# Linear attention and a mixture of experts on one core: the values' product folded into the heads' matrix

## The reference

```
q = xn @ Wq + bq;  k = xn @ Wk + bk;  v = xn @ Wv + bv
q = heads(q @ Wq2 + bq2);  k = heads(k @ Wk2 + bk2);  v = heads(v @ Wv2 + bv2)   # 16 heads of 8
q = elu(q) + 1;  k = elu(k) + 1
S = einsum('bhld,bhle->bhde', k, q)
out = einsum('bhmd,bhde->bhme', v, S)
qks = einsum('bhld,bhld->bhl', q, k) + 1e-6
out = out / qks[..., None]
out = layernorm(xn + out @ Wo + bo) * gamma + beta
# experts: 64 of them, 8 per token, at most 160 tokens each, and a shared one; swiglu with 384 inner units
logits = xn @ wg.T;  w, idx = top_k(softmax(logits), 8);  w /= sum(w)
y = sum over the chosen e of w_e * (x1 * silu(x2)) @ w2_e.T,  [x1, x2] = xn @ w1_e.T
```

## Time and profile before

| | |
|---|---|
| median of 3 runs | 354.65 us (354.23 to 355.87) |
| profiled execution's own time | 355.68 us |
| its span in the trace | 353.8 us |
| busy | PE 328.9 us (93%), DVE 281.6 (80%), ACT 194.8 (55%), POOL 251.5 (71%) |
| chain that ended last | PE 81%, DVE 8%, ACT 3%, issue 3%, DMA 2% |
| granted TensorE clock, mean | 0.992 |
| TensorE waits of L1280 (`up`) | 0.4 us in all, in g = 0, for the copy L609 of ScalarE |

### The profile page before, as it was taken

One profiled execution on the slowest core, in us unless ns is written; L12 is line 12 of the kernel. 1 busy time (PEld: TensorE's weight loads), 2 busy tenths in 40 slices (PEclk: granted clock), 3 DMA queues, 4 the chain that ended last, 5 costly groups with the idle time before them and its releaser, 6 DMA issues.

```text
span 353.8 us, 8965 instructions
## 1 busy us (share of the span) xinstructions
PE 328.9 (93%) x2944; PEld 314.2 (89%) x2944; DVE 281.6 (80%) x1134; ACT 194.8 (55%) x433; POOL 251.5 (71%) x258
## 2 busy tenths in 40 slices
PE   8899766999999999999999999999999999998880
PEld 8889665999999999999999999999999999997870
DVE  3898996887798989888888888898989886652595
ACT  3789622746565665757474746565665757343110
POOL 5687826158878878887888888877878886786200
PEclk9999999999999999999999999999999999999996
DMA  7997552499887778787868777887778787834598
GB/s 211 355 383 244 141 120 76 161 324 264 192 221 179 200 177 223 165 215 192 204 168 210 166 205 188 185 219 182 199 169 230 157 229 172 216 44 36 155 318 252
DMA packets 57054, 70.29 MB, mean 199 GB/s; under 512 B 11952, under 2 KB 44976, under 8 KB 57008
## 3 DMA queue, kind: packets, MB, share of 16 engines
q1 hardware_dynamic: 39536, 55.55, 50.4%
q0 software_dynamic: 15360, 13.12, 24.1%
q10 hardware_dynamic: 2112, 1.05, 1.0%
HBM read 54.26 MB, written 15.43 MB: 197 GB/s over the span
## 4 chain that ended last, share of the span: by engine, by line
PE 81%; DVE 8%; ACT 3%; issue 3%; DMA 2%; POOL 1%; SPq 1%; DVEq 0%; POOLq 0%
PE bank L1280 30%; PE bank L1290 12%; PE bank L1215 9%; PE bank L1224 5%; PE bank L1325 4%; PE bank L1299 4%; PE bank L1365 3%; PE bank L1331 2%; PE bank L1371 2%; PE bank L1346 2%; PE bank L1338 2%; PE bank L1254 1%; PE bank L1306 1%; DVE left L791 1%; PE bank L1239 1%
## 5 line engine op out<-in xcount | busy, mean ns | idle before, releaser
L515 POOL DMA_INDIRECT acc<-ys,idx_g x64 | 102.7, 1605 | 30.5 <-issue 15.4
L1280 PE MATMUL bank<-xe,ew 128*128 128x160 f32 x768 | 116.3, 301 | 0.4 <-ACT xe L609 0.4
L1280 PEld LDWEIGHTS bank<-xe,ew 128*128 128x128 f32 x768 | 107.4, 190 | 1.7 <-ACT xe L609 0.6
L496 POOL DMA_INDIRECT gath<-xng,idx_g x80 | 81.2, 1015 | 30.5 <-issue 27.3
L582 ACT ACTIVATE si<-bank 128x480 f32<-128x480 f32 (+1 forms) x96 | 52.1, 543 | 66.7 <-PE bank L1280 38.0
L1290 PE MATMUL bank<-ew,ac 128*128 128x128 f32 x384 | 53.4, 275 | 0.4 <-issue 0.4
L1290 PEld LDWEIGHTS bank<-ew,ac 128*128 128x128 f32 x384 | 49.5, 192 | 1.6 <-issue 0.8
L1215 PE MATMUL bank<-xT,shw 128*128 128x128 f32 x384 | 48.8, 276 | 0.1
L771 DVE TENSOR_TENSOR ac<-si,bank 128x480 f32<-128x480 f32 x64 | 40.9, 640 | 8.6 <-ACT si L582 5.2
L1215 PEld LDWEIGHTS bank<-xT,shw 128*128 128x128 f32 x384 | 45.6, 192 | 0.5 <-ACT si L582 0.3
L1224 PE MATMUL bank<-shw,acs 128*128 128x128 f32 x192 | 27.7, 280 | 6.8 <-DVE acs L762 4.1
(11 more groups left out here) (165 smaller groups left out, 613.5 us busy)
## 6 DMA issues: line engine op xcount, KB each, us to landing
ew<-in_expert_w SPq DMA_DIRECT2D x64, 384.0 KB, 3.6
ew<-in_expert_w SPq DMA_DIRECT2D x64, 192.0 KB, 2.9
ew<-acc SPq DMA_DIRECT2D x8, 512.0 KB, 7.9
x_sb<-in_x SPq DMA_DIRECT2D x8, 256.0 KB, 6.5
xng<-xn SPq DMA_DIRECT2D x8, 256.0 KB, 4.1
acc<-zeros SPq DMA_DIRECT2D x4, 512.0 KB, 4.3
acc<-betas SPq DMA_DIRECT2D x4, 512.0 KB, 3.0
gath<-xng,idx_g POOLq DMA_INDIRECT x80, 3.8
```

Of the source, the lines that this page charges most:

```text
L496: pool.indirect_dma_start(out=gath[:, p, m, :], out_offset=None, in_=xng, in_offset=bass.IndirectOffsetOnAxis(ap=idx_g[:, g % 4, m:m + 1], ...
L515: pool.indirect_dma_start(out=acc[adds_to[g, m]], out_offset=bass.IndirectOffsetOnAxis(ap=idx, axis=0), in_=src, in_offset=None, compute_o ...
L1280: last = pe.matmul(h_view(n, half_ + 1, CAP)[:, c, :], ew[p][m][:, k * P:(k + 1) * P], xe[:, p, m, :], start=True, stop=True)
```

## The change

The kernel no longer computes v. With C = Wv' S (Wv' the folded weights of v, S the heads' matrix) and c = S^T bvc, the attention output before the scaling, turned, is C^T xn^T + c. `fold_heads` therefore turns the inverses (which are spread to 8 columns for each head beforehand, `rq` of 128x256), multiplies `S_s` by the bias column and by the folded weights, all into `AV` (385 columns), and ScalarE's `heads_copy` takes them to `rC_s` in one copy. `attention_out` is then one product of 256 columns, and VectorE's scale adds c and multiplies by the turned inverses, writing `oT_s` directly. `values`, `out_T` and their two copies are gone. The folded value weights are stored turned. Places in the orders of TensorE, ScalarE and VectorE change with it.

```diff
-            def values_copy(a):
-
-                act.wait_ge(v_full, v_at['values', a] + 1)
-                if a > 0:
-                    act.wait_ge(q_full, q_at['out', a - 1] + 1)
-                act.activation(vT[:, :], AV[:, 0:L], ACT.Identity, bias=bvc[:, 0:1]).then_inc(v_done, 1)
-
-            def out_copy(a):
-
-                act.wait_ge(v_full, v_at['out T', a] + 1)
-                if a > 0:
-                    act.wait_ge(q_full, q_at['project', a - 1] + 1)
-                act.activation(oT_s[:, :], AV[:, 0:L], ACT.Copy).then_inc(v_done, 1)
+            def heads_copy(a):
+
+                act.wait_ge(v_full, v_at['fold', a] + 1)
+                act.activation(rC_s[:, :], AV[:, 0:L + D + 1], ACT.Copy).then_inc(v_done, 1)
...
             cum_copy(NR - 1)
-            values_copy(0)
             load_silu()
             silu(('s', 4))
             silu(('s', 5))
+            heads_copy(0)
+            silu(('s', 6))
             narrow_copy(1)
-            silu(('s', 6))
-            out_copy(0)
             silu(('s', 7))
...
-                if attend:
-                    values_copy(g + 1)
                 y_copy(g, 0)
...
                 silu(('s', EARLY + g))
+                if attend:
+                    heads_copy(g + 1)
                 if g + 2 < NG:
                     narrow_copy(g + 2)
                 silu(('e', g, 3))
-                if attend:
-                    out_copy(g + 1)
...
-                dve.reciprocal(rq[:, :, :], qks[:, :, :]).then_inc(rq_ready, 1)
+                if a > 0:
+                    dve.wait_ge(v_full, v_at['fold', a - 1] + 1)
+                dve.reciprocal(rq[:, :].rearrange("p (n d) -> p n d", d=DH),
+                               qks[:, :, :].rearrange("p j h -> p (j h)").unsqueeze(2).to_broadcast([P, TB * H, DH])).then_inc(rq_ready, 1)
...
                 dve.wait_ge(q_full, q_at['out', a] + 1)
-                dve.wait_ge(rq_ready, a + 1)
-                if a > 0:
-                    dve.wait_ge(v_full, v_at['out T', a - 1] + 1)
-                dve.tensor_tensor(o_s[:, :, :].rearrange("p j (h d) -> p (j h) d", h=H),
-                                  AQ[:, 0:TB * D].rearrange("p (n d) -> p n d", d=DH),
-                                  rq[:, :, :].rearrange("p j h -> p (j h)").unsqueeze(2).to_broadcast([P, TB * H, DH]),
-                                  ALU.mult).then_inc(q_done, 1)
+                dve.wait_ge(v_done, v_at['fold', a] + 1)
+                dve.scalar_tensor_tensor(oT_s[:, :], AQ[:, 0:L], rC_s[:, L + D:L + D + 1], rC_s[:, 0:L], ALU.add, ALU.mult).then_inc(q_done, 1)
...
-            attention_scale(0)
+            shared_mul(6)
+            shared_add(5)
             table_compare(1)
             table_tokens(1)
-            shared_mul(6)
-            shared_add(5)
+            attention_scale(0)
             shared_mul(7)
...
                 shared_mul(EARLY + g)
-                if a < B:
-                    attention_scale(a)
                 if g + 2 < NG:
                     table_compare(g + 2)
                 expert_mul(g, 3)
+                if a < B:
+                    attention_scale(a)
...
+            def fold_heads(a):
+
+
+                pe.wait_ge(rq_ready, a + 1)
+                pe.wait_ge(v_done, v_at['fold', a])
+                for j in range(TB):
+                    pe.transpose(AV[:, j * P:(j + 1) * P], rq[:, j * D:(j + 1) * D], ident)
+                pe.matmul(AV[:, L + D:L + D + 1], S_s[:, :], bvc[:, :], start=True, stop=True)
+                pe.matmul(AV[:, L:L + D], wqkv[:, 2 * D:3 * D], S_s[:, :], start=True, stop=True).then_inc(v_full, 1)
+
             def attention_out(a):
 
-                pe.wait_ge(v_done, v_at['kq', a] + 1)
+                pe.wait_ge(v_done, v_at['fold', a] + 1)
                 pe.wait_ge(q_done, q_at['out', a])
-                for j in range(TB):
-                    last = pe.matmul(AQ[:, j * D:(j + 1) * D], vT[:, j * P:(j + 1) * P], S_s[:, :], start=True, stop=True)
-                last.then_inc(q_full, 1)
...
+                pe.matmul(AQ[:, 0:L], rC_s[:, L:L + D], xT[:, a * L:(a + 1) * L], start=True, stop=True).then_inc(q_full, 1)
```

More of the change, by code:

```diff
@@ L63, in block_kernel @@
         q_uses += [('qk', g)] * (g > 0) + [('out', g), ('project', g)]
-        v_uses += [('values', g), ('kq', g), ('out T', g)]
+        v_uses += [('kq', g), ('fold', g)]
     a_uses += [('rest', NG - 1), ('sum', NG - 1)]
@@ L1193, in fold_weights @@
                 pe.matmul(Y[:, D:2 * D], wkT_s, w2_s[:, 1, :], start=True, stop=True)
-                pe.matmul(Y[:, 2 * D:3 * D], wvT_s, w2_s[:, 2, :], start=True, stop=True).then_inc(y_full, 1)
+                pe.matmul(Y[:, 2 * D:3 * D], w2_s[:, 2, :], wvT_s, start=True, stop=True).then_inc(y_full, 1)
             def fold_bias():
@@ L1326, in queries_keys @@
                 last.then_inc(full, 1)
-            def values(a):
-                pe.wait_ge(v_done, v_at['values', a])
-                pe.matmul(AV[:, 0:L], wqkv[:, 2 * D:3 * D], xT[:, a * L:(a + 1) * L], start=True, stop=True).then_inc(v_full, 1)
             def keys_queries(a):
@@ L1339, in keys_queries @@
                 last.then_inc(v_full, 1)
+            def fold_heads(a):
[5 more added lines that the diff above has]
+                pe.matmul(AV[:, L:L + D], wqkv[:, 2 * D:3 * D], S_s[:, :], start=True, stop=True).then_inc(v_full, 1)
             def attention_out(a):
-                pe.wait_ge(v_done, v_at['kq', a] + 1)
+                pe.wait_ge(v_done, v_at['fold', a] + 1)
                 pe.wait_ge(q_done, q_at['out', a])
-                for j in range(TB):
-                    last = pe.matmul(AQ[:, j * D:(j + 1) * D], vT[:, j * P:(j + 1) * P], S_s[:, :], start=True, stop=True)
-                last.then_inc(q_full, 1)
-            def out_T(a):
-                pe.wait_ge(q_done, q_at['out', a] + 1)
-                pe.wait_ge(v_done, v_at['out T', a])
-                for j in range(TB):
-                    last = pe.transpose(AV[:, j * P:(j + 1) * P], o_s[:, j, :], ident)
-                last.then_inc(v_full, 1)
+                pe.matmul(AQ[:, 0:L], rC_s[:, L:L + D], xT[:, a * L:(a + 1) * L], start=True, stop=True).then_inc(q_full, 1)
             def out_projection(a):
-                pe.wait_ge(v_done, v_at['out T', a] + 1)
                 pe.wait_ge(q_done, q_at['project', a])
@@ L1403, in _ @@
             pe.wait_ge(qk0_done, 1)
-            values(0)
             shared_up(4)
@@ L1409, in _ @@
             shared_down(4)
-            attention_out(0)
             shared_up(6)
             shared_down(5)
+            fold_heads(0)
             table(1)
-            out_T(0)
+            attention_out(0)
             shared_up(7)
@@ L1430, in _ @@
                     down_rest(g - 1)
-                if a < B:
-                    values(a)
                 down(g, 0)
@@ L1442, in _ @@
                 if a < B:
-                    attention_out(a)
+                    fold_heads(a)
                 if g + 2 < NG:
@@ L1447, in _ @@
                 if a < B:
-                    out_T(a)
+                    attention_out(a)
                 down(g, 2)
```

8 lines of the change are left out of this document (3 added, 5 removed).

## The result

The changed kernel takes 366.81 us (median of 4 runs, 366.42 to 368.29), the kernel before 355.1 us on the same chip (4 runs). The ratio is 1.0336, with a 95% interval of 1.0305 to 1.0367: **slower by 11.7 us** (366.81 - 355.1). The forecast was +9.9 us and 364.6 us. The profiled execution is the longest of the four, 368.29 us with a span of 366.5; the other three took 366.42 to 366.83.

A forecast was written before the change was run, and what follows sets the result against it. TensorE was taken to set the pace, VectorE's spare time being mostly unusable. Groups 2 to 13 add 8.5 us, g = 1 0.14, g = 0 0.57, prologue 0.66: +9.9 on 354.65, 364.6 us; range 359.5 to 369.

The forecast's parts named there:

- VectorE's gapless stretch: VectorE between `u1` and `S_s`: reciprocal 1.40 us longer, only 0.33 us idle, so TensorE waits 0.55 us before `fold_heads`.
- Rival (d): Reciprocal with broadcast source: 8.4 ns per element, +0.55 us each over the forecast, +7.1 in all, 371.7 us; 5 in 100.
- The chain behind F, through copy, table and scale: From the first product after `shared_up` to the next output projection: TensorE needs 4.14 us, then waits a second time, 0.17.
- TensorE saves nothing: TensorE's work per group: value product saves 0.44 us, `fold_heads` and the 256-column product add it back; sum -0.01 us.
- The prediction's step for the period: Time between output projection starts in groups 2 to 13: 17.28 instead of 16.57 us, +0.71, twelve times, 8.5 us.
- (a): VectorE absorbs the longer reciprocal in its idle time; only prologue and g = 0 lose: +1.2 us, 355.9; 5 in 100.
- (b): Wide reciprocal on VectorE costs no more than another operation of 256 elements: together +1.3 us, 355.9; 5 in 100.
- (c): Cheap reciprocal, and the single-column product hides its loads: TensorE needs 0.21 us less per group, 350.4 us; 5 in 100.
- Groups 14 and 15 have no table or no attention: nothing.: Last two passes of the expert-group loop: the change was to add no time there, 0 us.
- the prediction's own sign: Check on the last two groups, 14 and 15: their periods must be what they were before the change.
- The sum: Whole kernel: 8.5 for groups 2 to 13, 0.14 in g = 1, 0.57 in g = 0, 0.66 in prologue: 9.9 us.

The follow-up runs named there:

- experiment 1: Changed kernel with the reciprocal back at 128x32 and a ScalarE copy spreading it to 128x256: 358.84 us, ratio 1.0088 to the kernel before.
- experiment 3: Changed kernel with the scale moved ahead of expert_mul(g,3), wide reciprocal left: 365.25 us, ratio 1.0264 to the kernel before.
- 8: Changed kernel with `finish(g-2)`, four VectorE operations, moved ahead of `queries_keys`' first operation, into VectorE's idle time: 373.52 us, ratio 1.0357.
- 9: Repeats on other chips: `finish` moved 372.47 us; both repairs 361.46; both without the single-column product 359.13; small inverse spread by ScalarE 367.7 (1.0253).
- experiment 6: Changed kernel with both repairs, small inverse spread by ScalarE and scale ahead of expert_mul(g,3): 362.68 us, ratio 1.0046; repeated 361.46 us, 1.0062.
- experiment 4: Changed kernel with a second 128x256 reciprocal into a buffer that nobody reads: 410.7 us, ratio 1.1532 to the kernel before.

## Why the prediction was right, and what it missed

**VectorE's gapless stretch: right, shown.** The reciprocal's price of 1.75 us came out to the nanosecond, its place in the stretch between `u1` and `S_s` gave F = P + 13.04 for 12.97, and taking it out (experiment 1) brought F back and 0.54 us per pass with it. Rival (d) read the repeat count of 8 that the Trainium skill gives a reciprocal (VectorE: DVE Perf Modes, the section on the fixed hardware budget) as eight steps of 1.05 ns. That reading is not borne out: 6.25 ns per element, six such steps, holds from 4 to 256 elements.

**The chain behind F, through copy, table and scale: right, shown.** It was put at 4.31 and took 4.34; moving the scale (experiment 3) took 0.18 back, forecast 0.17. That holds where the copy `nar` comes 0.28 us behind the table, as it does in every pass of the loop in this trace; where it comes later, as in 8 and 9, the chain is longer, and the prediction has no term for that.

**TensorE saves nothing: right, shown.** With all waits gone a pass takes 16.66 against 16.57 (experiment 6), and the single column is 0.23 us for 0.21. What the sum of -0.01 us doesn't tell is where the work lies: 0.34 us less ahead of F (12.86 to 12.52, forecast 0.44) and 0.43 more behind it. With F held by `S_s` the first is lost and the second is paid. So the 0.80 us are 0.17 by which F is later than before, 0.43 of TensorE's work behind it and 0.20 of the late scale. The prediction's step for the period has this in its numbers, but doesn't say it.

**The rivals.** (a) fell: VectorE had 1.86 us of idle time left in the pass (17.38 - 15.52) and could not use it. (b), (c) and (d) fell with the 1753 ns, (c) also with the 0.23 us of the single column.

**What was too small.** The step "The period is 17.28 instead of 16.57: +0.71 us" measured +0.80 in the usual pass (17.37). In the pass shown F is 0.07 late, 0.04 of it between `S_s` and the fold (177.01 to 177.44, 0.43 for 0.39), and the part behind F is 0.03 longer, where the scale's 0.48 in place of 0.42 is partly made up elsewhere. In g = 7 and 8 the period was 17.51 and 17.75: a small VectorE operation took longer (L947 0.31 and 0.48 us instead of 0.17), and no idle time is left before `S_s` to take it up. Together +10.2 for 8.5.

**The step that failed** is "Groups 14 and 15 have no table or no attention: nothing." g = 14 lost 0.62 us. It has no table, but the stretch from `u1` to `S_s` needs none: in the timeline above `expert_mul(14,1)` waits 0.64 us for `silu`, which stands behind ScalarE's exponentials, and from L923 to L957 it is 7.88 us, as in the other passes. I had read the table's operations as what fills the stretch; it is as long without them. So F is held by `S_s` here too (a wait of 0.33 us), at P + 13.02 for 12.86, and behind it TensorE has its added work, 3.75 us for 3.29. With the small inverse of experiment 1 all but 0.09 of the 0.62 is gone. By the prediction's own sign, that the periods of groups 14 and 15 must be what they were, this part was wrong.

**The sum.** 0.71 + 0.62 + 0.09 + 10.20 + 0.62 = 12.2 for 9.9, with the tail's -0.8 that is 11.4. The medians say 11.7. The forecast of 9.9 was too small by 1.8 us, nearly all of it in g = 2 to 14; the tail's 0.8, which was not forecast either, makes up part of it by luck.

None of the versions beats the kernel before. The nearest that computes all of it is 6, at 1.0046 and 1.0062.

## What to carry to other kernels

Price an iterative operation such as the reciprocal by its own slope over sizes that the trace holds, before writing it out to a broadcast shape: eight times the elements was five times the time. Idle time on an engine counts only where the added work can start in it; look for the gapless stretch that the added operation falls into, and for the lead that its result has. A saving ahead of a wait and a cost behind it don't cancel, though their sum is nothing. And an fp32 product of one column with its own weight load cost as much here as one of 128 columns (0.23 and 0.22 us), so count products, not columns.

## What the runs showed of the hardware

The granted clock fell to half behind a wait of 1.96 us on TensorE in experiment 4, and 1.67 us of added work cost 3.07 us per pass; it stayed at 1.00 behind waits of 0.35 and 1.15 us. An effect measured by adding a cost can so turn out larger than the cost.

The hand-over from TensorE to a small ScalarE copy took 0.28 us on one chip and 0.90 on another, in the same kernel, and its ratio went from 1.0088 to 1.0253 with it. The cause is open, and on one chip both were seen, in different kernels. The changed kernel itself ran on one chip only, with the copy at 0.28, so its 11.7 us are the price where that copy is on time. The kernel before itself lay between 354.65 and 361.42 us on the chips of these runs, but the ratio takes that out. A comparison of two versions with 1% between them needs both on one chip, and better on two.
